# Cross-attention and a quantised feed-forward layer on one core: last four tiles fed through the score banks with VectorE's help, weights transposed by transfers, later loads of x and biases, 24 idle transposes near the close

## The reference

```python
def read(query, mem):                      # query = layernorm(x)
    q = query @ Wq.T + bq;  k = mem @ Wk.T + bk;  v = mem @ Wv.T + bv
    scores = (q @ k.T) / 16
    keep the 32 largest of each row, softmax over them
    return (attn @ v) @ Wo.T + bo
def bitlinear(x, w, b):
    x = x * rsqrt(mean(x*x) + 1e-5)
    xq = round(x * 127/max|x|) / (127/max|x|)      # per row
    wq = round(clip(w / mean|w|, -1, 1)) * mean|w|  # ternary
    return xq @ wq.T + b
x = x + read(layernorm(x), ctx)
h = gelu(bitlinear(layernorm(x), w1, b1))          # 256 -> 1024
x = x + bitlinear(h, w2, b2)                       # 1024 -> 256
```

## Time and profile before

| | us |
|---|---|
| median of 3 runs | 296.18 |
| lowest and highest of them | 294.36, 296.98 |
| the profiled execution, its own time | 295.05 |
| its span, first to last instruction | 293.2 |

### The profile page before, as it was taken

One profiled execution on the slowest core, in us unless ns is written; L12 is line 12 of the kernel. 1 busy time (PEld: TensorE's weight loads), 2 busy tenths in 40 slices (PEclk: granted clock), 3 DMA queues, 4 the chain that ended last, 5 costly groups with the idle time before them and its releaser, 6 DMA issues. The chain is left out here.

```text
span 293.2 us, 5370 instructions
## 1 busy us (share of the span) xinstructions
PE 266.3 (91%) x1520; PEld 230.1 (78%) x1528; DVE 224.3 (76%) x968; ACT 223.4 (76%) x337; POOL 177.9 (61%) x243
## 2 busy tenths in 40 slices
PE   7799999999999899999999999989999999765644
PEld 7699998999787788788879787869788877453233
DVE  2563597897988898889988999798989889765351
ACT  2457768463679978996999699959997997396781
POOL 4104881600789669856985698559856766267610
PEclk9999999999999999999999999999999999999577
DMA  6971000002000320042004200520041007000411
GB/s 225 342 267 36 3 16 21 2 1 72 3 1 2 89 55 0 10 120 56 1 18 125 38 1 18 132 35 2 18 100 27 2 19 127 1 1 0 107 36 38
DMA packets 27245, 15.91 MB, mean 54 GB/s; under 512 B 18381, under 2 KB 26126, under 8 KB 27214
## 3 DMA queue, kind: packets, MB, share of 16 engines
q1 hardware_dynamic: 26510, 14.50, 19.1%
q0 software_dynamic: 272, 0.79, 0.9%
q10 hardware_dynamic: 432, 0.26, 0.3%
HBM read 9.77 MB, written 2.10 MB: 40 GB/s over the span
## 5 line engine op out<-in xcount | busy, mean ns | idle before, releaser
L396 PE MATMUL bank<-vo,pT 128*128 128x257 f32 (+1 forms) x416 | 99.2, 382 | 3.7 <-ACT pT L1090 3.7
L396 PEld LDWEIGHTS bank<-vo,pT 128*128 128x128 f32 (+1 forms) x416 | 75.8, 190 | 16.4 <-ACT pT L1090 7.0
L862 POOL TENSOR_TENSOR g<-g,b_bc 128x512 f32<-128x512 f32 x32 | 48.9, 1544 | 23.8 <-ACT g L1117 23.8
L1410 DVE MAX8 cand<-s_sb 128x8 f32<-128x50 f32 (+1 forms) x512 | 60.7, 201 | 2.7 <-ACT s_sb L1040 2.1
L244 PE MATMUL score<-k_high,q_low 128*128 128x400 f32 (+1 forms) x128 | 50.7, 396 | 0.0
L244 PE MATMUL score<-k_low,q_high 128*128 128x400 f32 (+1 forms) x128 | 44.3, 346 | 0.0
L244 PE MATMUL score<-k_high,q_high 128*128 128x400 f32 (+1 forms) x128 | 44.1, 344 | 0.0
L1090 ACT ACTIVATE pT<-bank 128x512 f32<-128x512 f32 x64 | 32.1, 517 | 8.4 <-PE bank L252 8.2
L1040 ACT ACTIVATE s_sb<-score 128x400 f32<-128x400 f32 x64 | 30.9, 504 | 6.5 <-PE score L244 6.4
L1445 DVE SCALAR_TENSOR_TENSOR e_all<-s_sb,best,e_all 128x1601 f32<-128x1601 f32 x16 | 33.9, 2117 | 1.8 <-ACT e_all L1082 1.7
L252 PE MATMUL bank<-ident,e_all 128*128 128x128 f32 (+1 forms) x208 | 31.6, 274 | 3.3 <-ACT pT L1090 1.7
(11 more groups left out here) (145 smaller groups left out, 507.4 us busy)
## 6 DMA issues: line engine op xcount, KB each, us to landing
x_in<-in_x SPq DMA_DIRECT2D x16, 128.0 KB, 2.3
w_sb<-in_L_ffn_w SPq DMA_DIRECT2D x2, 1024.0 KB, 13.1
x_res<-in_x SPq DMA_DIRECT2D x16, 128.0 KB, 2.4
out<-o_sb SPq DMA_DIRECT2D x16, 128.0 KB, 1.9
ctx_sb<-in_ctx SPq DMA_DIRECT2D x3, 512.0 KB, 6.3
b_bc<-in_L_ffn_b POOLq DMA_DIRECT2D x1, 512.0 KB, 8.4
w_q<-in_L_xattn_Wq SPq DMA_DIRECT2D x1, 256.0 KB, 3.1
w_k<-in_L_xattn_Wk ACTq DMA_DIRECT2D x1, 256.0 KB, 4.1
```

Of the source, the lines that this page charges most:

```text
L396: ins = pe.matmul(bank[:, 0:DV], pT[0:n, t % 2, b * P:(b + 1) * P], vo[0:n, b, :], start=(b == 0), stop=(b == SB - 1))
L862: pool.tensor_tensor(g[:, u, part], g[:, u, part], b1_bc[:, part], ALU.add).then_inc(biased, 1)
L1410: ins = dve.max(cand[:, t % 2, k:CAND:PIECES], s_sb[:, t % 2, k * PIECE:end])
```

## The change

*Banks.* The four score banks join `banks` as a third group, `LATE`. Tiles 12 to 15 use it for `up`, `turn_y2` and `down`, and 14 and 15 for `turn_y1_tile`; a bank's first use there waits until the last scores in it are copied.

*Close.* y2 of tiles 12 and 13 is turned by PE, no longer by a transfer; ACT and DVE copy one half each (`take_y2`). For tiles 12 to 15 DVE does scale and bias in one instruction (`hidden` on DVE) in place of ACT and POOL. Tiles 14 and 15 keep their hidden layer in `s_sb`, with gelu, maximum and rounding in halves, rounding and copies divided between ACT and DVE. Before the turns of y2 of 14 and 15 PE does 24 transposes whose result nobody reads (`hold_clock`).

*Weights.* `turn_w1`, `turn_w2`, `take_w1` and `take_w2` go. ACT lowers the rounded weights to bfloat16 (`lower_weights`) into `y2` and `o_sb`, which are free then, and SP turns each with one transfer of 2048 columns.

*Loads.* x of pair 0 is issued after the context; b1 and b2 once the context has landed; residuals of x one place earlier in SP's list.

*Order.* All five lists are written anew, in prologue, loop and close.

```diff
-        banks = [stack.enter_context(nc.psum_tensor(f"bank{k}", [P, BANK], F32)) for k in range(4)]
-        EARLY, TURN, RESULT = (0, 1, 2, 3), (0, 1), (2, 3)
+        banks = [stack.enter_context(nc.psum_tensor(f"bank{k}", [P, BANK], F32)) for k in range(4)] + score
+        EARLY, TURN, RESULT, LATE = (0, 1, 2, 3), (0, 1), (2, 3), (4, 5, 6, 7)
...
             if uses[k]:
                 nc.tensor.wait_ge(drained[k], uses[k])
+            elif k in LATE:
+                nc.tensor.wait_ge(s_copied, TILES * SC - SC + k - LATE[0] + 1)
...
+            def hold_clock(n):
+                bank = banks[place["still"][0]] if "still" in place else fill("still", TURN)
+                for _ in range(n):
+                    pe.transpose(bank[:, 0:P], ident[:, :], ident[:, :])
...
+            def turn_ffn_weights(k):
+                sp.wait_ge(weights_lowered, k + 1)
+                if k == 0:
+                    sp.dma_start_transpose(w1T[:, :, :, :].rearrange("p b c n -> p (b c) n"),
+                                           y2[:, :, :].rearrange("p a b -> p (a b)")).then_inc(weights_turned[0], 16)
...
+            def load_ffn_biases():
+                pool.wait_ge(ctx_in[(SB - 1) // CTX_PIECE], 16)
+                pool.dma_start(b1_bc[:, :], b1.partition_broadcast(P)).then_inc(ffn_bias_in, 16)
+                pool.dma_start(b2_bc[:, :], b2.partition_broadcast(P)).then_inc(ffn_bias_in, 16)
...
+            def hidden(t, h):
...
+                src = wait_full(dve, ("up", t, h))
+                drain(dve.scalar_tensor_tensor(hidden_of(t)[:, part], src[:, :], row1[:, t // 2 % 2, 6, u:u + 1], b1_bc[:, part],
+                                               ALU.mult, ALU.add), ("up", t, h))
...
+            def quantise_half(t, h):
...
+                dve.tensor_scalar(y2_raised[:, u, part], hidden_of(t)[:, part], row2[:, t // 2 % 2, 5, u:u + 1], MAGIC,
+                                  ALU.mult, ALU.add).then_inc(last_raised[h], 1)
```

ACT's loop, before and now, from `exp_all` of the odd tile to that of the next even one:

```diff
-                    hidden(2 * r - 2, 1)
-                    copy_scores(2 * r + 2, 0)
-                    copy_scores(2 * r + 2, 1)
-                    gelu(2 * r - 2)
-                    hidden(2 * r - 1, 0)
...
-                    take_weights(2 * r + 1, 0)
-                    gelu(2 * r - 1)
+                    hidden(2 * r - 2, 0)
+                    copy_scores(2 * r + 2, 0)
+                    hidden(2 * r - 2, 1)
+                    hidden(2 * r - 1, 0)
+                    gelu(2 * r - 2)
+                    copy_scores(2 * r + 2, 1)
...
+                    gelu(2 * r - 1)
+                    take_weights(2 * r + 1, 0)
```

More of the change, by code:

```diff
@@ L416, in up @@
                 if t == 0:
-                    for k in range(4):
-                        wait_drained(pe, ("w1", k))
-                bank = fill(("up", t, h), RESULT)
+                    pe.wait_ge(weights_turned[0], 16)
+                bank = fill(("up", t, h), RESULT if t < LAST - 2 else LATE)
                 u = t % 2
                 for c in range(DC):
-                    ins = pe.matmul(bank[:, :], y1T[:, c, u * P:(u + 1) * P], w1T[:, c, h * BANK:(h + 1) * BANK],
+                    ins = pe.matmul(bank[:, :], y1T[:, c, u * P:(u + 1) * P], w1T[:, h * 4:h * 4 + 4, c, :],
                                     start=(c == 0), stop=(c == DC - 1))
@@ L438, in down @@
                 if t == 0:
-                    for k in range(4):
-                        wait_drained(pe, ("w2", k))
-                bank = fill(("out", t), RESULT)
+                    pe.wait_ge(weights_turned[1], 16)
+                bank = fill(("out", t), RESULT if t < LAST - 2 else LATE)
                 u = t % 2
                 for b in range(FB):
-                    ins = pe.matmul(bank[:, 0:D], y2T[:, u, b, :], w2T[:, b, :],
+                    ins = pe.matmul(bank[:, 0:D], y2T[:, u, b, :], w2T[:, :, b, :],
                                     start=(b == 0), stop=(b == FB - 1))
@@ L950, in _ @@
+            row_scales_1(2)
+            quantise_1(2, 0)
+            quantise_1(2, 1)
+            split_queries(4)
+            add_bias(4, 0)
+            add_bias(4, 1)
+            normalise_scale(5)
+            add_bias(5, 0)
+            add_bias(5, 1)
+            normalise(5, 0)
+            row_scales_2(2)
+            for r in range(3):
+                if live(r + 1):
+                    keep_residual(r + 1, 1)
                 if live(r + 3):
                     residual(2 * r + 7)
-                if live(r + 5):
-                    normalise_scale(r + 5)
@@ L1145, in quantise_2 @@
                                bias=magic_col[:, 0:1]).then_inc(y2_ready, 1)
+            def quantise_half(t, h):
+                u, part = t % 2, slice(h * BANK, (h + 1) * BANK)
+                act.wait_ge(last2_step[u], 6)
+                for k in range(2):
+                    wait_full(act, ("y2", t - 2, k))
+                act.activation(y2_raised[:, u, part], hidden_of(t)[:, part], ACT.Identity, scale=row2[:, t // 2 % 2, 5, u:u + 1],
+                               bias=magic_col[:, 0:1]).then_inc(last_raised[h], 1)
             def lower_2(t):
@@ L1514, in centre, with tile_scales @@
                                   apply_absolute_value=True).then_inc(x2_step[u], 1)
-            def tile_scales(row, v, u, done, largest, mean):
+            def tile_scales(row, v, u, done, largest, other, mean):
                 n = [2]
@@ L1692, in _ @@
             count(14)
-            centre(12)
-            output(8)
             weigh(14)
             largest_count(14)
+            output(8)
             release(14)
@@ L1706, in _ @@
             best_8(15, 0)
+            next_8(15, 1)
             output(10)
-            next_8(15, 1)
-            output(11)
             next_8(15, 2)
             next_8(15, 3)
-            attended(14)
             count(15)
             weigh(15)
+            output(11)
+            hidden(12, 0)
+            largest_count(15)
+            hidden(12, 1)
+            release(15)
+            hidden(13, 0)
+            attended(14)
             moments(14)
-            largest_count(15)
-            release(15)
             centre(14)
+            hidden(13, 1)
+            gelu_max(12)
             tile_spread_1(14)
-            gelu_max(12)
+            gelu_max(13)
             tile_scales_1(14)
-            gelu_max(13)
             quantise_1(14)
```

620 lines of the change are left out of this document (331 added, 289 removed).

## The result

| | before | after |
|---|---|---|
| median, us | 296.06 (4 runs) | 285.52 (4 runs) |
| lowest and highest | 294.36, 296.98 | 285.15, 287.63 |
| profiled execution, own time and span | 295.05, 293.2 | 285.15, 283.3 |

The ratio is 0.965, with a 95% interval of 0.961 to 0.970. The change takes away 10.5 us where 14.0 was forecast; the time stands inside the range, 3.3 us above the forecast.

What follows compares the result with a forecast made beforehand. The prediction took PE's own work to bound the middle and a chain of few instructions over engines the close. Gains of 4.0 + 2.5 + 7.5 = 14.0 us from the median 296.18 gave 282.2 us, range 277.5 to 288.5.

Steps and rivals of the forecast that it cites:

- Start and weights: Prologue: context wait gone (1.7), PE's weight transposes gone (2.8), 0.9 lost to later tile 1 release; 4.0 us taken, bounds 2 and 4.6.
- All on the engine that bounds: Prologue: PE loses 8 groups of 4 weight transposes at 0.35 us each, 2.8 us, all counted as gain on PE.
- The order in the rounds: Middle: the new order removes half of PE's 4.9 us of waits, 2.5 us; bounds 4.9 and a loss of 2.
- gelu is fed sooner: Rounds: two first halves of hidden go ahead, covering POOL's bias addition; the exponential starts some 0.6 us earlier.
- The sign called wrong in advance: Middle: pairs of 28.5 us or more would show the forecast wrong; 27.9 to 28.2 would show it right.
- The close: Last tiles: earlier tile 15 and a shorter chain make 9.4 us, less 1.5 for hand-overs; 7.5 taken, bounds 3 and 9.4.
- (b): Close: DVE's first step on tile 15's result to its last output falls from 24.3 to 16.9 us, 7.4 less.
- (a): Close: PE's 1.71 us wait for ACT goes; tile 15's products start and end about 2.0 us earlier.
- 24 idle transposes: Close, between down(13) and y2(14)'s first turn: they hold full clock and are free, 2.6 us in a 3 us gap.
- My third rival: Idle transposes do not hold the clock, the close runs at half clock: gain 10.5, so 285.7 us; chance 0.10.
- The first: Rival: DVE becomes the bound, the middle gives nothing and the close half; gain 9, so 287.2 us; chance 0.20.
- The slower one: Rival: PE waits each round for a weight copy behind gelu; decides from 2.1 us a round, 300.8 at 2.3; chance 0.03.

Runs made afterwards that it cites:

- copy_first: Changed kernel with ACT copying the second chunk of scores ahead of gelu and DVE taking its candidates ahead of gelu's maximum: 283.22 us, ratio 0.957.
- old_all: Changed kernel's start and close with the old order of rounds on all five engines, POOL's from its first round on: 283.46 us, ratio 0.957.
- no_hold: Changed kernel without its 24 idle transposes, nothing else different: 287.36 us, ratio 0.971.
- before_hold: Kernel before with only 24 idle transposes added at each of two places of its close: 293.23 us against 297.06, ratio 0.986.

## Why the prediction was right or wrong

**Start and weights, 4.0 forecast, 4.05 measured: right in the sum, by luck, and wrong in its terms.** The wait for context is gone, as forecast at 1.7. But DVE's masking of tile 0 already leads by 3.73 us (41.47 against 37.74), and in the kernel before PE's first weight transposes (40.54) came behind all scores of tile 0, so they have no part in that. PE's first scores of tile 0, before and after:

```profile
31.99 0.34 PE L244 MATMUL score<-k_high,q_low 128*128 128x400 f32 x1
```

```profile
28.49 0.34 PE L257 MATMUL score<-k_high,q_low 128*128 128x400 f32 x1
```

They come 3.50 us earlier: 1.74 is the wait, and 1.43 the value block 3 that stood ahead of them (30.56 to 31.99) and now stands behind. The prediction named this move and put it at nothing. The transposes it put at 2.8, with 0.9 taken back for a longer masking of tile 1; that masking did grow by 1.0 us (1.88 to 2.92), but that of tile 0 shrank by 1.6 (3.51 to 1.88), which the prediction left out. From the masking of tile 0 to the first y1 it takes 36.66 us before and 36.34 after: with all eight groups gone, and the rest reordered, 0.3 less. "All on the engine that bounds" was the step that failed: PE bounds the middle, not this stretch, where it waits for DVE's release instead (1.6 us, 0.2 before). This is read from two traces; no run took it apart.

**The order in the rounds, 2.5 forecast, -3.3 measured: wrong in sign, and outside my bound of -2.** The step that failed: "gelu is fed sooner (...), so POOL's bias addition is covered, and I work out the exponential to start some 0.6 us earlier". The exponential starts 0.3 us earlier (15.5 us behind the copy of y1 instead of 15.8). Gelu is not fed sooner: POOL's first addition begins 3.40 us behind the copy of y1 as before, and gelu gains 0.13. The additions meet the masking of the odd tile, a contention of which the prediction had a row of its own and used it only in the prologue; that meeting was there before. New is that x2b holds up the even tile's masking. I also looked at ACT alone. The copy of the second chunk of scores went behind gelu, and DVE needs it; nothing in the prediction asked what DVE does meanwhile. The sign called wrong in advance (pairs of 28.5 or more) showed up at 29.1. Of the 0.8 us between 29.15 and 28.35, copy_first shows 0.5 to hang on these two exchanges; that most of the 0.5 goes through a shorter second meeting is read from its trace. The other 0.3 is argued, not shown: against old_all, copy_first is 0.4 us shorter ahead of the even masking (17.13 against 17.57) and 0.7 longer behind it (11.42 against 10.76). The masking itself is 0.1 of the 0.7; an output that now stands ahead of the centring of the odd tile, and the centring of the even one (0.62 us against 0.33), are candidates for the rest.

**The close, 7.5 forecast, 9.26 measured: right in kind, 1.76 short.** (b) The chain from tile 15's result to the last output was put at 16.9 + 1.5 = 18.4 and is 18.0, a gain of 6.2. (a) The earlier start of tile 15 was put at 2.0 and is 3.0 (266.76 - 263.02 = 3.74, less the lead of 0.73). PE's wait of 1.71 us is not gone but 1.01 us long; most of (a) comes from the last round before the close, which the two kernels take 32.0 and 30.1 us for. That the time fell inside the range although the rounds left theirs is in part luck: this surplus took back 1.8 of the 5.8 us that the rounds were off.

**24 idle transposes: right.** Clock 1.0 to the last product, 24 of them in 2.78 us, in a gap of 2.82. Without them it falls. The Trainium skill, "TensorE: Matmul & The Clock Gate", Part 4, would have had the 24 make no difference; no_hold (1.8 us, and a clock of 0.50 in place of 1.00) and before_hold (3.8 us) say otherwise, and the measurement decides. My third rival falls: its price, 3.5 us, was twice what no_hold shows.

**The rivals.** The third, "idle transposes do not hold the clock", came nearest in time (285.7 against 285.52), by accident, since the clock was held. The first, "the middle gives nothing and the close half" (287.2), was nearer to what happened, but not right either: the middle gave less than nothing, the close more than all. (The slack of DVE that it was weighed against, "3 us of 30", is 3.9 by the earlier trace rows.) The slower one named a stall of PE behind gelu in each round, decisive from 2.1 us; the place was right, gelu behind POOL in ACT's queue, but who stands behind it is DVE, and the round loses 0.7.

## What to carry to other kernels

When an order is changed, follow in the queue of each engine what is now behind the moved instruction, and for whom it is meant: here two pairs of calls in exchanged places, one on ACT and one on DVE, cost 2.3 us, though PE was the busiest engine all along. In a tuned pipeline the lists of the engines are one thing; judge a mixture by the length of its settled rounds before its total is believed. Where the path ends in a chain with PE idle, try idle transposes in its gaps before anything cleverer: that alone gave 3.8 us of 297 here. And see which of two changes at the start stands ahead of the gain: here, by the traces, a value block moved behind the first scores accounts for more of it than eight groups of transposes taken out.

## What the runs showed of the hardware

Idle float32 transposes count for the clock: the granted clock stayed at 1.00 with 24 of them in the gap and fell to 0.50 without; in the kernel before, 48 in the close raised its mean over the execution (0.958 to 0.974 without, 0.988 to 0.992 with them). A POOL addition of two tensors and DVE's masking exclude one another: two additions of 1.26 us take 3.98 when they begin 0.3 us behind the masking, and the masking takes 2.34 instead of 1.89 when one of 0.72 us begins 0.06 us ahead of it, 2.94 when one of 1.27 us begins 0.01 us ahead. I had expected a slowdown of both, not a queue of one behind the other. No engine of the kernel after waited for the transfers of 2048 columns that turn the weights.
